# A new order of steps inside a pair of attention units, and 512-column matmuls ahead of the scores in two attentions

## The chip, the cores and the metric

One core of a Trainium2 chip. The metric is the device time in microseconds of one launch of the whole program; for the kernel before it is the median of three runs. TensorE has two levels of clock, 1.2 and 2.4 GHz. The profile gives the granted clock as a share of full speed: 0.50 is 1.2 GHz throughout, 1.00 is 2.4 GHz throughout.

## The reference, cut to what matters

The program is a vision tower in float32: 32 images of 37 tokens (36 patches and one class token), 192 channels, 12 heads. Tokens go through a patch embedding and four layers:

```python
h = _L0_tok_ref(x, ...)                                   # patches @ W + b + pos, class token
h = _layernorm(h + _L0_attn_ref(h, ...))                  # attention whose scores are mixed with their neighbours
h = _layernorm(h + _L0_ffn_ref(h, ...))                   # causal attention, then 8 experts with a capacity
h = _layernorm(h + _L1_attn_ref(h, ...))                  # attention without its diagonal, + h
h = _layernorm(h + _L1_ffn_ref(h, ...))                   # four T5 layers
...
for i in range(L):                                        # L = 4, H = 12, DK = 64
    nx = t5_layer_norm(h, ln1[i])
    q, k, v = nx @ attn_q[i], nx @ attn_k[i], nx @ attn_v[i]
    attn = jax.nn.softmax(q @ k.T + bias, axis=-1)        # for each head
    h = h + (attn @ v) @ attn_o[i]
    nx = t5_layer_norm(h, ln2[i])
    y = relu(nx @ ffn_wi[i]) @ ffn_wo[i]                  # layers 1 and 3 add 2 of 8 experts
    h = h + y
```

So there are seven attentions in a row of twelve stages: one with neighbours, one causal, one without the diagonal (heads of 16 channels each), and four T5 attentions (heads of 64 channels).

## The kernel before, in words

The tokens are cut into 11 groups of three images (111 tokens, `TG`). Stages follow each other as `att 0`, `att 1` (causal), `ffn 0`, `att 2` (diagonal), then four times `att`, `ffn` for T5. Four engines run the same list of steps, `PROGRAM`, each doing its own part of a step: TensorE (PE) its matmuls, VectorE (DVE), ScalarE (ACT) and GpSimd (POOL) what follows. Each engine works through its part strictly in the order of that list and waits on semaphores for the others. So the place of a step in the list sets what stands behind what on every engine. The list is written out by functions; `att_order` (line 276) makes it for all attentions but the first.

In an attention the twelve heads of a group are cut into four units of three heads, and two units make a pair; there are 22 pairs in a stage. The steps are:

- `S` (scores of a pair): PE fills both banks of `ps_score` (line 1042, and in the causal and the diagonal attention a mask by a bfloat16 matmul at line 1037). DVE then shifts each unit: in T5 it adds the bias (line 1423), takes the negated maximum (1425) and adds it (1426). The result is in `prob`.
- `E`: ACT applies the exponential to `prob` (line 1246), both units of the pair, one after the other.
- `PT`: PE transposes a unit of `prob` into the single bank `ps_pt` (line 983), ACT copies it to `probt` (line 1251).
- `PV`: PE multiplies the pair's `probt` by `v` into `ps_o` (line 1064); DVE divides (lines 1440 and 1444) into `o`.
- `OT` and `Y`: the transposed output (line 1073, copy by ACT at line 1230) and its projection (line 1084, DVE adds it to `x` and starts a norm, which POOL ends, lines 1321 to 1351).
- `A`: PE transposes the normed rows (line 887, in the diagonal attention 881), ACT rounds them (lines 1183, 1184), DVE makes the low part (lines 1513, 1516).
- `QK` and `V`: projections from the split input, five matmuls each (lines 1009 and 1022), copied out by ACT (lines 1216 and 1223). `QK` is made for a block of three groups at once: 336 columns.

`ps_proj` has two banks, which `QK`, `V`, `OT` and `Y` take in turn.

`att_order` is a pipeline over pairs. For pair n it lists the scores of n, the exponentials of n, the two transposes of pair n-1, and the `PV` of pair n-2. All other steps of the group (`att_fill`, line 225) are a flat list that is spread evenly over the gaps behind `E`, each `PT` and `PV`:

```python
steps += [("S", g, p), ("E", g, p)]
steps += [("PT", h, 2 * q), ("PT", h, 2 * q + 1)]
steps.append(("PV", *divmod(n - 2, 2)))
```

A `W1` step (a weight load of the next stage, rounded by ACT and split by DVE) and the gathers of an expert stage before (`GAT` on POOL, `COMB` on DVE) are among the fill.

Of the kernel before, what the change touches and what calls it, by code (L numbers as in the profile page):

```python
# [8 lines left out]
ACT = mybir.ActivationFunctionType  # L9
# [23 lines left out]
E = 8  # L33
# [188 lines left out]
    return out  # L222


def att_fill(a, g, last_stage, follower):

    s = ATTS[a]
    ffn_next = follower[0] == "ffn"
    fill = []
    if last_stage in COMBINED and g < G:  # L230
        for c in (3 + 2 * g, 4 + 2 * g):
            if c < G:
                fill.append(("prev", ("COMB", c)))
                if c + GAT_RING < G:
                    fill.append(("prev", ("GAT", c + GAT_RING)))
    if g < G:
        b = BLOCK_OF[g]
        i = g - BLOCKS[b][0]
        if b + 1 < NB:
            g0, n = BLOCKS[b + 1]  # L240
            if i == 1:
                fill += [("A", x) for x in range(g0 + 2, g0 + n)]
                fill += [("QK", b + 1, j) for j in range(s.qk // 2)]
            elif i == 2:
                fill += [("QK", b + 1, j) for j in range(s.qk // 2, s.qk)]
    if 2 <= g:
        fill.insert(0, ("OT", g - 2, s.vparts - 1))
    if g + 1 < G:
        fill += [("V", g + 1, j) for j in range(s.vparts)]
    if 2 <= g:  # L250
        fill.append(("Y", g - 2))
    if a == DIAG and g >= 3:
        fill.append(("N2", g - 3))
    if ffn_next and 3 <= g < G:
        fill.append(("next", ("A", g - 3)))
        if follower[1] in SPARSE and g >= 4:
            fill.append(("next", ("L", g - 4)))
            if g >= 5:
                fill.append(("next", ("CNT", g - 5)))
    if g < G and i == 0 and b + 1 < NB:  # L260
        fill += [("A", x) for x in range(g0, min(g0 + 2, g0 + n))]
    if not ffn_next and g == G - 1:
        fill += [("next", ("A", x)) for x in range(3)]
    if not ffn_next and g == G:
        fill += [("next", x) for x in first_block(follower[1])]
    r = LOAD0[follower]
    if a == DIAG:
        fill += {2: [("W1", r)], 9: [("W1", r + 1)], 10: [("W1", r + 2)]}.get(g, [])
    elif g == (2 if a == CAUSAL else 9):
        fill.append(("W1", r))  # L270
    if s.t5 and 1 <= g:
        fill.append(("OT", g - 1, 0))
    return fill


def att_order(a, last_stage, follower):

    out = first_block(a) if last_stage[0] == "ffn" else []
    pairs = 2 * G
    for n in range(pairs + 2):  # L280
        g, p = divmod(n, 2)
        if p == 0:
            fill = att_fill(a, g, last_stage, follower)
            count, given, gap = len(fill), 0, 0
# [8 lines left out]
        for x in steps:  # L293
            out.append(x)
            if x[0] == "S":
                continue
            gap += 1
            upto = min(-(-count * gap // 8), count)
            out += fill[given:upto]
            given = max(given, upto)  # L300
        if p == 1:
            out += fill[given:]
            given = count
    last = ATTS[a].vparts - 1
    out += fill[given:] + [("OT", G - 1, last), ("Y", G - 1)]
    if a == DIAG:
        out += [("N2", g) for g in range(G) if ("N2", g) not in out]
    return out
# [226 lines left out]
def tower(nc, patches, tok_w, consts, young, rows, gains, gates_w, head_scale, bias_src, edge,  # L535
          aw_neigh, wo_all, w1_all, w2_all, out, rows_in, rows_out):
    with ExitStack() as ctx:
# [306 lines left out]
        def _(pe):  # L844
# [141 lines left out]
            def att_step(st, step):  # L986
# [39 lines left out]
                elif kind == "S":  # L1026
# [137 lines left out]
        def _(act):  # L1164
# [33 lines left out]
            for st, step in PROGRAM:  # L1198
# [35 lines left out]
                elif kind == "E":  # L1234
                    _, g, u = step
                    a = st[1]
                    for e in range(1 if a == NEIGH else 2):
                        v = u if a == NEIGH else 2 * u + e
                        n = SCORE[(st, "S", g, u) if a == NEIGH else (st, "S", g, u, e)]

                        if ATTS[a].t5:
                            act.wait_ge(shifted, unit(a - T5, g, v) + 1)
                        else:
                            act.wait_ge(score_taken[n % 2], n // 2 + 1)
                        at = unit(a, g, v) % 4
                        act.activation(prob[:, at, :, :], prob[:, at, :, :], ACT.Exp).then_inc(prob_ready, 1)  # L1246
                elif kind == "PT":
                    _, g, u = step
                    n = unit(st[1], g, u)
                    act.wait_ge(pt_full, n + 1)  # L1250
                    act.activation(probt[:, n % 4, :, :], ps_pt[0:TG, 0:3 * TG].rearrange("p (c n) -> p c n", c=3),  # L1251
                                   ACT.Copy).then_inc(pt_taken, 1)
                elif kind == "GATE":
                    gates += 1
                    act.wait_ge(gap_ready, gates)
                    act.activation(egap[:], gap[:], ACT.Exp).then_inc(egap_ready, 1)
                elif kind == "U":
                    bank, taken = take_proj(key)
                    _, i, m = step
                    b = FFN[st[1]][i]  # L1260
                    n = DISPATCH[st[1]].width if b.tile is not None else b.groups[1] * TP
                    act.activation(hid[:, i % 2, m, 0:n], bank[:, 0:n],  # L1262
                                   ACT.Relu if b.tile is None else ACT.Gelu).then_inc(taken, 1)
                elif kind == "X":
                    turned_rows(st, step[1])
                elif kind == "W1":
                    r = step[1]
                    act.wait_ge(w1_raw, 16 * (r + 1))
                    if r >= W_RING:

                        act.wait_ge(proj_full, LAST_PROJ[r - W_RING] + 1)
                    act.activation(w1_hi[:, r % W_RING, :, :], w1_in[:], ACT.Copy).then_inc(w1_rounded, 1)  # L1272
# [589 lines left out]
```

## Time and profile before

| what | value |
|---|---|
| median of 3 runs | 2679.45 us (2669.82 to 2680.93) |
| profiled execution, its own time | 2659.68 us |
| its span | 2657.7 us |
| granted TensorE clock, mean | 0.752 |
| PE busy | 2016.8 us (76%) |
| DVE busy | 1135.4 us (43%) |
| ACT busy | 801.1 us (30%) |
| POOL busy | 727.2 us (27%) |

The profile lists, for stretches of the span, the busy time of each engine and the granted clock; for an engine, how long it sat idle and which instruction ended that; and the instructions in order of time. The name behind an arrow is what the engine had waited for. Engines overlap, so busy shares do not add up to the span.

### The profile page before, as it was taken

The numbers are of one execution on the slowest core, as the hardware profiler recorded it, in microseconds if no ns is written. First come the engines' busy times: TensorE is split into PE (matmuls) and PEld (weight loads), VectorE is DVE, ScalarE is ACT, GpSimd is POOL, SyncE is SP. The second block draws the span as 40 slices with busy tenths as digits, with TensorE's granted clock in tenths as the row PEclk, the third lists the DMA queues.
The fourth block names the chain that finished last, engine by engine and source line by source line (L and its number), as shares of the span: only waits on it lengthen the run. The fifth ranks groups of instructions, "written<-read, shape, count | busy, mean of one in ns | idle before, by whom it ended". The sixth has DMA issues, their size and how long they took to land.

```text
span 2657.7 us, 35685 instructions
## 1 busy us (share of the span) xinstructions
PE 2016.8 (76%) x12440; PEld 1851.9 (70%) x12440; DVE 1135.4 (43%) x3201; ACT 801.1 (30%) x1907; POOL 727.2 (27%) x1831
## 2 busy tenths in 40 slices
PE   7984888868388767778777789966777967778991
PEld 7983777768267666668666788855666866778891
DVE  2531434443344434444445543434444444454436
ACT  1221332223122233233333234422332333324440
POOL 3561412220553421125212220044211611131003
PEclk8795555579555577678877699987767988769995
DMA  3094000035000000001000036630000100004651
GB/s 100 17 286 143 1 12 8 14 94 167 23 15 1 25 9 1 1 13 34 12 1 11 11 124 199 195 98 11 1 1 13 45 1 1 11 11 157 200 165 42
DMA packets 77414, 151.03 MB, mean 57 GB/s; under 512 B 6345, under 2 KB 56627, under 8 KB 77142
## 3 DMA queue, kind: packets, MB, share of 16 engines
q1 hardware_dynamic: 70902, 136.49, 16.3%
q0 software_dynamic: 6336, 12.26, 1.6%
q8 instruction: 103, 1.69, 0.3%
q14 instruction: 73, 0.59, 0.1%
HBM read 108.67 MB, written 41.05 MB: 56 GB/s over the span
## 4 chain that ended last, share of the span: by engine, by line
PE 45%; DVE 21%; issue 18%; ACT 5%; POOL 5%; DMA 3%; SPq 2%; DVEq 0%; POOLq 0%; ACTq 0%
PE ps_proj L1009 8%; PE ps_o L1064 7%; PE ps_proj L1084 6%; DVE prob L1426 5%; DVE negmax L1425 5%; PE ps_score L1042 4%; PE ps_score L1155 4%; PE ps_pt L983 3%; DVE prob L1423 3%; PE ps_proj L1138 3%; PE ps_proj L1022 2%; ACT prob L1246 2%; PE ps_proj L936 2%; DMA w_in<-w_all_dram 2%; SPq L812 2%
## 5 line engine op out<-in xcount | busy, mean ns | idle before, releaser
L1321 POOL TENSOR_SCALAR tmp<-rs,var 111x1 f32<-111x1 f32 x462 | 168.1, 364 | 1218.5 <-DVE rs L1397 1187.2
L983 PE MATMUL ps_pt<-const,prob 111*111 111x111 f32 x924 | 208.6, 352 | 161.8 <-ACT probt L1251 161.2
L1246 ACT ACTIVATE prob<-prob 111x333 f32<-111x333 f32 x308 | 148.0, 481 | 591.2 <-DVE prob L1426 591.2
L1155 PE MATMUL ps_score<-w,hid 128*112 128x192 f32 (+2 forms) x1680 | 309.0, 336 | 10.6 <-DVE x L1700 6.2
L983 PEld LDWEIGHTS ps_pt<-const,prob 111*111 111x111 f32 x924 | 176.6, 252 | 185.0 <-ACT prob L1246 176.2
L1155 PEld LDWEIGHTS ps_score<-w,hid 128*112 128x112 f32 (+2 forms) x1680 | 280.3, 182 | 13.2 <-DVE x L1700 7.5
L1064 PEld LDWEIGHTS ps_o<-v,probt 111*111 111x111 f32 x1584 | 250.2, 251 | 3.3 <-issue 2.6
L1064 PE MATMUL ps_o<-v,probt 111*111 111x65 f32 (+1 forms) x1584 | 247.7, 316 | 0.0
L1262 ACT ACTIVATE hid<-ps_proj 128x224 f32<-128x224 f32 (+2 forms) x360 | 134.1, 382 | 262.9 <-PE ps_proj L1138 262.8
L1309 POOL DMA_INDIRECT tin<-rows_out,idx x66 | 67.2, 1018 | 495.1 <-issue 385.0
L1084 PE MATMUL ps_proj<-wo,ot 128*111 128x192 f32 (+1 forms) x616 | 165.3, 427 | 25.9 <-ACT ot L1230 13.8
L1251 ACT ACTIVATE probt<-ps_pt 111x333 f32<-111x333 f32 x308 | 137.5, 446 | 137.3 <-PE ps_pt L983 134.2
L1042 PE MATMUL ps_score<-qk 64*111 64x111 f32 (+1 forms) x1584 | 154.7, 346 | 23.6 <-DVE prob L1423 13.6
L1009 PE MATMUL ps_proj<-xa_hi,w_hi 128*128 128x336 f32 (+1 forms) x240 | 112.3, 468 | 79.4 <-DVE xb L1516 41.1
L1042 PEld LDWEIGHTS ps_score<-qk 64*111 64x111 f32 (+1 forms) x1584 | 125.6, 239 | 61.6 <-issue 57.9
L1084 PEld LDWEIGHTS ps_proj<-wo,ot 128*111 128x111 f32 (+1 forms) x616 | 133.1, 237 | 41.9 <-issue 24.8
L1425 DVE TENSOR_REDUCE negmax<-ps_score 111x3 f32<-111x333 f32 x132 | 66.6, 504 | 210.0 <-PE ps_score L1042 131.2
L1216 ACT ACTIVATE qk<-ps_proj 128x336 f32<-128x336 f32 (+1 forms) x228 | 96.5, 425 | 191.7 <-PE ps_proj L1009 191.7
L1440 DVE RECIPROCAL rden<-ps_o 111x6 f32<-111x6 f32 (+1 forms) x121 | 24.9, 206 | 286.6 <-PE ps_o L1064 275.5
L1322 POOL TENSOR_SCALAR tmp<-tmp,rs 111x1 f32<-111x1 f32 x462 | 133.2, 288 | 46.9
L1272 ACT ACTIVATE w_hi<-w_in 128x1536 fp32r<-128x1536 f32 x66 | 97.9, 1483 | 115.6 <-DMA w_in<-w_all_dram 115.6
L1536 DVE TENSOR_TENSOR w_lo<-w_in,w_hi 128x768 fp32r<-128x768 f32 x66 | 63.8, 966 | 155.7 <-ACT w_hi L1272 155.5
(214 smaller groups left out, 4444.9 us busy)
## 6 DMA issues: line engine op xcount, KB each, us to landing
w_in<-w_all_dram SPq DMA_DIRECT2D x66, 768.0 KB, 4.4
w<-w_all_dram SPq DMA_DIRECT2D x50, 576.0 KB, 5.0
rows_in<-w_lo SPq DMA_DIRECT2D x1, 12320.0 KB, 62.6
rows_out<-w_lo SPq DMA_DIRECT2D x1, 9240.0 KB, 85.7
tin<-rows_in SPq DMA_DIRECT2D x36, 224.0 KB
rows_out<-tout SPq DMA_DIRECT2D x36, 168.0 KB
patch<-patches_dram SPq DMA_DIRECT2D x11, 333.0 KB, 3.0
wo<-wo_all_dram SPq DMA_DIRECT2D x6, 576.0 KB, 3.9
```

The source lines that it names most:

```text
L983: last = pe.transpose(ps_pt[0:TG, i * TG:(i + 1) * TG], prob[:, n % 4, i, :], ident)
L1009: last = pe.matmul(bank[:, 0:n * TP], w[:, slot, c, at:at + 128], src, start=(i == 0), stop=(i == len(terms) - 1))
L1042: ins = pe.matmul(bank[0:TG, i * TG:(i + 1) * TG], qk[at:at + s.rows, b % 2, c, t0:t0 + TG], qk[at:at + s.rows, b % 2, s.chunks + c, t0:t0 ...
L1064: last = pe.matmul(ps_o[0:TG, h // 6, col:col + s.d + 1], probt[:, unit(a, g, u) % 4, i, :], v[:, g % 3, h, :], start=True, stop=True, ski ...
L1084: last = pe.matmul(bank[0:TG, 0:C], ot[0:n, g % 2, c, :], w[0:n, c, :], start=(c == 0), stop=(c == len(parts) - 1))
L1155: last = pe.matmul(bank[0:n, 0:C], hid[:, i % 2, m, at:at + n], w2[:, slot, m, :], start=(m == 0), stop=(m == FC - 1))
L1246: act.activation(prob[:, at, :, :], prob[:, at, :, :], ACT.Exp).then_inc(prob_ready, 1)
L1251: act.activation(probt[:, n % 4, :, :], ps_pt[0:TG, 0:3 * TG].rearrange("p (c n) -> p c n", c=3), ACT.Copy).then_inc(pt_taken, 1)
L1262: act.activation(hid[:, i % 2, m, 0:n], bank[:, 0:n], ACT.Relu if b.tile is None else ACT.Gelu).then_inc(taken, 1)
L1321: link(pool.tensor_scalar(t, r, r, v, ALU.mult, ALU.mult))
L1322: link(pool.tensor_scalar(t, t, -3.0, r, ALU.add, ALU.mult))
L1425: link(dve.tensor_reduce(negmax[:], scores, AX.X, ALU.max, negate=True))
```

## The change

Two things.

The order inside a pair is rewritten, for the six attentions from the causal one on. `att_fill` no longer returns a flat list, it returns six named slots for a group (three for each of its two pairs), and each fill step has its fixed slot. `E` is now a step of a single unit. For pair n the list now reads: scores of n; first transpose of n-1; slot; second transpose of n-1; slot; first exponential of n; `PV` of n-2; slot; second exponential of n.

And in the causal attention (all groups) and the diagonal one (groups 0 to 8), PE runs four matmuls of 128 x 512 ahead of each pair's scores, and twelve ahead of the first pair's. They read a ready weight block of the next stage and write the first score bank, whose content the mask matmul then overwrites. That makes 2 x 12 + 38 x 4 = 176 of them; nothing reads what they compute.

```diff
+COMB_AT = {0: ((3, 0), (4, 2)), 1: ((5, 1), (6, 5)), 2: ((7, 3),), 3: ((8, 1),), 4: ((9, 1),), 5: ((10, 1),)}
...
 def att_fill(a, g, last_stage, follower):
...
+    slots = [[] for _ in range(6)]
+    if 2 <= g:
+        slots[0].append(("OT", g - 2, s.vparts - 1))
     if g < G:
...
         if b + 1 < NB:
             g0, n = BLOCKS[b + 1]
+            if i == 0:
+                slots[3].append(("A", g0))
             if i == 1:
-                fill += [("A", x) for x in range(g0 + 2, g0 + n)]
-                fill += [("QK", b + 1, j) for j in range(s.qk // 2)]
-            elif i == 2:
-                fill += [("QK", b + 1, j) for j in range(s.qk // 2, s.qk)]
+                for k, x in zip((0, 3), range(g0 + 1, g0 + n)):
+                    slots[k].append(("A", x))
+            if i:
+                sixth = s.qk // 6
+                for k, slot in enumerate((4, 5) if i == 1 else (1, 2, 4, 5)):
+                    first = (k if i == 1 else k + 2) * sixth
+                    slots[slot] += [("QK", b + 1, j) for j in range(first, first + sixth)]
+    if g + 1 < G:
+        for j in range(s.vparts):
+            slots[(1, 4)[j]].append(("V", g + 1, j))
     if 2 <= g:
-        fill.insert(0, ("OT", g - 2, s.vparts - 1))
...
+        slots[2].append(("Y", g - 2))
...
     if s.t5 and 1 <= g:
-        fill.append(("OT", g - 1, 0))
-    return fill
+        slots[5].append(("OT", g - 1, 0))
+    return slots
...
-        steps = []
+            slots = att_fill(a, g, last_stage, follower)
         if n < pairs:
-            steps += [("S", g, p), ("E", g, p)]
-        if 1 <= n <= pairs:
-            h, q = divmod(n - 1, 2)
-            steps += [("PT", h, 2 * q), ("PT", h, 2 * q + 1)]
+            out.append(("S", g, p))
+        for k in range(2):
+            if 1 <= n <= pairs:
+                h, q = divmod(n - 1, 2)
+                out.append(("PT", h, 2 * q + k))
+            out += slots[3 * p + k]
+        if n < pairs:
+            out.append(("E", g, 2 * p))
         if n >= 2:
-            steps.append(("PV", *divmod(n - 2, 2)))
...
+            out.append(("PV", *divmod(n - 2, 2)))
+        out += slots[3 * p + 2]
+        if n < pairs:
+            out.append(("E", g, 2 * p + 1))
...
+DENSE = {CAUSAL: 4, DIAG: 4}
...
+                    if a in DENSE and g < (9 if a == DIAG else G):
+
+                        full = w1_hi[:, LOAD0[st] % W_RING, :, :].rearrange("p c n -> p (c n)")
+                        for _ in range(DENSE[a] * (3 if p == 0 and g == 0 else 1)):
+                            pe.matmul(banks[0], full[:, 0:128], full[:, 0:512], start=True, stop=True,
+                                      skip_group_check=True)
```

In the changed kernel lines are shifted: the scores are line 1050, the transposes 985, the exponential 1252, the copy of a transpose 1257, the block transpose's rounding 1191 and 1192, the copies of `ot`, `v` and `qk` 1238, 1231 and 1224; the added matmuls are line 1041.

How ACT's order moves, in the first T5 attention, from the last pair of group 2 into group 3. Before:

```order
L1251 ACTIVATE probt<-ps_pt 111x333
L1230 ACTIVATE ot<-ps_proj 128x333
L1246 ACTIVATE prob<-prob 111x333 x2
L1230 ACTIVATE ot<-ps_proj 128x333
L1251 ACTIVATE probt<-ps_pt 111x333
L1223 ACTIVATE v<-ps_proj 111x6x64
L1251 ACTIVATE probt<-ps_pt 111x333
L1223 ACTIVATE v<-ps_proj 111x6x64
L1246 ACTIVATE prob<-prob 111x333 x2
```

The same place in the changed kernel:

```order
L1238 ACTIVATE ot<-ps_proj 128x333
L1252 ACTIVATE prob<-prob 111x333
L1257 ACTIVATE probt<-ps_pt 111x333
L1238 ACTIVATE ot<-ps_proj 128x333
L1257 ACTIVATE probt<-ps_pt 111x333
L1231 ACTIVATE v<-ps_proj 111x6x64
L1252 ACTIVATE prob<-prob 111x333 x2
```

Before, both exponentials of the new pair stand ahead of the two copies of transposes and of what lies between them; now they stand behind.

How PE's order moves, in the causal attention, at the first pair of group 2. Before:

```order
L1064 MATMUL ps_o<-v,probt 111x17 x6
L1037 MATMUL ps_score<-maskb,identb 111x333 x2
L1042 MATMUL ps_score<-qk 111x111 x6
L1073 MATMUL ps_proj<-const,o 128x111
L1073 MATMUL ps_proj<-const,o 64x111
L983 MATMUL ps_pt<-const,prob 111x111 x3
```

The same place in the changed kernel:

```order
L1041 MATMUL ps_score<-w_hi 128x512 x4
L1045 MATMUL ps_score<-maskb,identb 111x333 x2
L1050 MATMUL ps_score<-qk 111x111 x6
L985 MATMUL ps_pt<-const,prob 111x111 x3
L1081 MATMUL ps_proj<-const,o 128x111
L1081 MATMUL ps_proj<-const,o 64x111
L985 MATMUL ps_pt<-const,prob 111x111 x3
```

The four new matmuls stand right ahead of the mask, and the first transpose is moved to stand right behind the scores, ahead of the output transposes.

## Rows read from the trace of the kernel before

**Rows 1.** The page: PE's busy share, and its granted clock in 40 slices.
```profile
PE 2016.8 (76%) x12440; PEld 1851.9 (70%) x12440; DVE 1135.4 (43%) x3201; ACT 801.1 (30%) x1907; POOL 727.2 (27%) x1831
...
PEclk8795555579555577678877699987767988769995
```

**Rows 2.** Stretches by attention: start:end, length, busy per engine, clock, DMA share, GB/s.
```profile
302.00:530.00 228.00, 190.71 (x1002) 162.43 (x1002) 92.42 (x300) 62.66 (x172) 57.20 (x141) 0.54 0.03 10
700.00:925.00 225.00, 179.33 (x939) 147.81 (x937) 103.33 (x294) 64.84 (x164) 102.10 (x275) 0.54 0.03 9
943.00:1190.00 247.00, 172.67 (x1074) 157.93 (x1073) 104.12 (x258) 75.94 (x192) 43.19 (x121) 0.73 0.02 6
1275.00:1525.00 250.00, 180.53 (x1175) 165.99 (x1172) 120.08 (x340) 79.10 (x198) 51.32 (x125) 0.77 0.02 6
1785.00:2040.00 255.00, 177.03 (x1073) 162.10 (x1072) 115.77 (x298) 77.75 (x192) 68.94 (x184) 0.73 0.02 7
2125.00:2375.00 250.00, 181.93 (x1175) 167.28 (x1172) 120.10 (x340) 79.13 (x198) 50.77 (x124) 0.76 0.02 6
```

**Rows 3.** Who PE waited for, 302 to 2375 us: total, times, longest.
```profile
PE ps_pt L983 <- ACT probt L1251: 112.3, 53, 6.0
PE ps_turn L887 <- POOL xn L1351: 58.4, 13, 11.7
PE ps_proj L1009 <- DVE xb L1516: 41.1, 13, 4.5
...
PE ps_proj L1009 <- ACT ot L1230: 37.1, 18, 2.7
PE ps_proj L1022 <- ACT qk L1216: 29.6, 17, 2.2
...
PE ps_proj L1084 <- ACT ot L1230: 13.1, 10, 2.7
PE ps_proj L1084 <- ACT v L1223: 12.1, 6, 2.0
...
PE ps_proj L1022 <- ACT ot L1230: 5.2, 4, 1.8
```

**Rows 4.** Timeline, one pair of the first T5 attention: start, duration, engine, instruction, idle before.
```profile
1009.04 0.84 PE L1042 MATMUL ps_score<-qk 64*111 64x111 f32 x12
...
1011.85 0.48 ACT L1246 ACTIVATE prob<-prob 111x333 f32<-111x333 f32 x1 [2.25 <-DVE prob L1426]
...
1013.46 0.48 ACT L1246 ACTIVATE prob<-prob 111x333 f32<-111x333 f32 x1 [1.13 <-DVE prob L1426]
...
1014.18 0.44 ACT L1251 ACTIVATE probt<-ps_pt 111x333 f32<-111x333 f32 x1
...
1014.76 0.87 PE L983 MATMUL ps_pt<-const,prob 111*111 111x111 f32 x3 [2.78 <-ACT probt L1251]
```

**Rows 5.** Timeline of PE: the same matmuls at either clock, start and duration.
```profile
1388.82 0.32 PE L1009 MATMUL ps_proj<-xb,w_hi 128*128 128x336 f32 x1
1388.98 0.32 PE L1009 MATMUL ps_proj<-xb,w_lo 128*128 128x336 f32 x1
...
1389.81 0.48 PE L1009 MATMUL ps_proj<-xb,w_hi 128*128 128x336 f32 x1
1390.09 0.48 PE L1009 MATMUL ps_proj<-xb,w_lo 128*128 128x336 f32 x1
...
1393.31 1.29 PE L1064 MATMUL ps_o<-v,probt 111*111 111x65 f32 x12
```

**Rows 6.** Timeline of PE: `PV` of a T5 pair at the low clock.
```profile
1032.78 2.37 PE L1064 MATMUL ps_o<-v,probt 111*111 111x65 f32 x12
```

**Rows 7.** Stretches of 50 us: first attention, first expert stage, second T5 attention.
```profile
250.00:300.00 50.00, 50.00 (x228) 46.02 (x229) 18.25 (x56) 11.11 (x30) 23.58 (x68) 0.50 0.00 1
...
600.00:650.00 50.00, 48.14 (x329) 47.82 (x326) 18.45 (x31) 21.35 (x40) 0.00 (x0) 1.00 0.51 165
...
1300.00:1350.00 50.00, 35.63 (x243) 32.66 (x239) 21.16 (x51) 16.26 (x40) 7.52 (x21) 0.85 0.00 1
```

More of the change, by code:

```diff
@@ L228, in att_fill @@
     ffn_next = follower[0] == "ffn"
[L229 to L235, printed above, removed]
+    slots = [[] for _ in range(6)]
+    if 2 <= g:
+        slots[0].append(("OT", g - 2, s.vparts - 1))
     if g < G:
@@ L240, in att_fill @@
             g0, n = BLOCKS[b + 1]
+            if i == 0:
+                slots[3].append(("A", g0))
             if i == 1:
-                fill += [("A", x) for x in range(g0 + 2, g0 + n)]
-                fill += [("QK", b + 1, j) for j in range(s.qk // 2)]
-            elif i == 2:
-                fill += [("QK", b + 1, j) for j in range(s.qk // 2, s.qk)]
-    if 2 <= g:
-        fill.insert(0, ("OT", g - 2, s.vparts - 1))
-    if g + 1 < G:
-        fill += [("V", g + 1, j) for j in range(s.vparts)]
@@ L250, in att_fill @@
-    if 2 <= g:
-        fill.append(("Y", g - 2))
+                for k, x in zip((0, 3), range(g0 + 1, g0 + n)):
[8 more added lines that the diff above has]
+            slots[(1, 4)[j]].append(("V", g + 1, j))
@@ L252, in att_fill @@
+    if 2 <= g:
+        slots[2].append(("Y", g - 2))
+    if last_stage in COMBINED and g < G:
+        for c, k in COMB_AT.get(g, ()):
+            slots[k].append(("prev", ("COMB", c)))
+            if c + GAT_RING < G:
+                slots[k].append(("prev", ("GAT", c + GAT_RING)))
     if a == DIAG and g >= 3:
-        fill.append(("N2", g - 3))
+        slots[4].append(("N2", g - 3))
     if ffn_next and 3 <= g < G:
-        fill.append(("next", ("A", g - 3)))
+        slots[3].append(("next", ("A", g - 3)))
@@ L256, in att_fill @@
         if follower[1] in SPARSE and g >= 4:
-            fill.append(("next", ("L", g - 4)))
+            slots[2].append(("next", ("L", g - 4)))
             if g >= 5:
-                fill.append(("next", ("CNT", g - 5)))
-    if g < G and i == 0 and b + 1 < NB:
-        fill += [("A", x) for x in range(g0, min(g0 + 2, g0 + n))]
+                slots[5].append(("next", ("CNT", g - 5)))
     if not ffn_next and g == G - 1:
-        fill += [("next", ("A", x)) for x in range(3)]
+        for x in range(3):
+            slots[1 + x].append(("next", ("A", x)))
@@ L264, in att_fill @@
     if not ffn_next and g == G:
-        fill += [("next", x) for x in first_block(follower[1])]
+        slots[3] += [("next", x) for x in first_block(follower[1])]
     r = LOAD0[follower]
     if a == DIAG:
-        fill += {2: [("W1", r)], 9: [("W1", r + 1)], 10: [("W1", r + 2)]}.get(g, [])
+        slots[5] += {2: [("W1", r)], 9: [("W1", r + 1)], 10: [("W1", r + 2)]}.get(g, [])
     elif g == (2 if a == CAUSAL else 9):
-        fill.append(("W1", r))
+        slots[5].append(("W1", r))
     if s.t5 and 1 <= g:
-        fill.append(("OT", g - 1, 0))
@@ L282, in att_order @@
         if p == 0:
-            fill = att_fill(a, g, last_stage, follower)
-            count, given, gap = len(fill), 0, 0
-        steps = []
+            slots = att_fill(a, g, last_stage, follower)
         if n < pairs:
-            steps += [("S", g, p), ("E", g, p)]
-        if 1 <= n <= pairs:
-            h, q = divmod(n - 1, 2)
-            steps += [("PT", h, 2 * q), ("PT", h, 2 * q + 1)]
-        if n >= 2:
-            steps.append(("PV", *divmod(n - 2, 2)))
[L293 to L303, printed above, removed]
+            out.append(("S", g, p))
[6 more added lines that the diff above has]
+            out.append(("E", g, 2 * p))
+        if n >= 2:
+            out.append(("PV", *divmod(n - 2, 2)))
+        out += slots[3 * p + 2]
+        if n < pairs:
+            out.append(("E", g, 2 * p + 1))
     last = ATTS[a].vparts - 1
-    out += fill[given:] + [("OT", G - 1, last), ("Y", G - 1)]
+    out += [("OT", G - 1, last), ("Y", G - 1)]
     if a == DIAG:
@@ L1236, in _ @@
                     a = st[1]
[L1237 to L1246, printed above, removed]
+                    n = SCORE[(st, "S", g, u) if a == NEIGH else (st, "S", g, u // 2, u % 2)]
+                    if ATTS[a].t5:
+                        act.wait_ge(shifted, unit(a - T5, g, u) + 1)
+                    else:
+                        act.wait_ge(score_taken[n % 2], n // 2 + 1)
+                    at = unit(a, g, u) % 4
+                    act.activation(prob[:, at, :, :], prob[:, at, :, :], ACT.Exp).then_inc(prob_ready, 1)
                 elif kind == "PT":
```

## The prediction

> **What bounds the kernel now.** I read the share of the engines and the clock first, then the attentions one by one, then who PE waits for in them, then one pair in order of time. The page: PE is busy for 2016.8 us of 2657.7, and no other engine for half of it, so PE and its waits set the end; its clock dips in exactly the slices that hold attentions [rows 1]. The stretches: the causal and the diagonal attention take 228 and 225 us, with PE busy for 190.71 and 179.33 at a granted clock of 0.54, that is almost wholly at 1.2 GHz. The four T5 attentions take 247, 250, 255 and 250 us; PE is busy for 172.67, 180.53, 177.03 and 181.93 at 0.73 to 0.77 [rows 2]. Together these six stretches are 1455 us, with PE idle for 83.0 us in the first two (453.0 less 370.0) and 289.8 in the other four (1002.0 less 712.2). Two things are to be had there: the idle time, and the half speed.
>
> The waits: of the idle time the largest single one is PE's transposes waiting for ACT's copy of the one before, 112.3 us. With the other waits that ACT ends (37.1, 29.6, 13.1, 12.1 and 5.2) it makes 209.4 us [rows 3]. ACT is not busy at all: 76 to 79 us of 250 [rows 2]. The pair in order of time says why. The scores start at 1009.04. ACT's next instruction in its list is the exponential, which it can start only at 1011.85 and, for the second unit, at 1013.46, since DVE must shift both units first. The copy of a transpose that had long been there follows at 1014.18, and PE, with its two projection banks full and its one transpose bank occupied, sits idle for 2.78 us until 1014.76 [rows 4]. So in each pair ACT's queue stands for some 4 us behind exponentials that nobody needs yet (they are used one pair later).
>
> **The change part by part.**
>
> *The exponentials.* Copies of transposes, of `qk`, `v` and `ot` that PE needs at once now stand ahead of them. The first exponential comes after two transposes and two slots, the second after `PV` and another slot. By then DVE has done its shift in most pairs (4.4 us from the start of the scores to the second exponential [rows 4]), and if not, PE has that much work ahead of it. A wait of ACT costs PE only when two more projections pile up. What stays: the second transpose still needs the copy of the first (0.44 us [rows 4] and the way there and back), and a slot between them is sometimes empty or a short `OT`. I take four fifths of the 209.4 us: **168 us**. The bounds are 0, if the exponential only blocks at its new place, and 209.
>
> *The other moved steps.* A group's first pair has `OT`, `V` and `Y`, its second `A`, `V`, `OT`. `QK` was halved over the second and third group of a block; now the third has two thirds, the second one third, the first none, as before. `A` of a block's last group stands one slot ahead of the first `QK`, which needs DVE's low part, and DVE has the pair's two shifts ahead of it. That wait is there already (41.1 us in 13 waits), as is the one for POOL's norms (58.4 in 13) [rows 3]; I leave both as they are. The gathers, the combining steps behind an expert stage and the weight loads keep their groups and move by at most a group's worth; POOL (102.10 of 225 us in its fullest stretch [rows 2]) and SP's queue have room.
>
> *The T5 clock.* A dense PE should be granted the high clock for longer. What it is worth: five matmuls of 336 columns follow each other at 0.28 us at the low clock and at 0.16 at the high one; a `PV` takes 2.37 us and 1.29 [rows 5, 6]. So at full clock PE needs 0.55 of its time at the low one. A granted share c is a share 2c - 1 of the time at the high clock; the time factor is 1 - 0.45(2c - 1). At today's mean, 0.75, it is 0.78. I take 0.92 for a PE without its ACT waits (factor 0.62), since 0.85 is had now in a stretch where PE is busy for 35.63 of 50 us [rows 7]. Busy time goes from 712 to 570: **142 us** less. Bounds: 0 (the clock stays) and 208 (1.00 throughout).
>
> *The 176 dense matmuls.* By 512/336 of those distances one costs 0.43 us at the low clock and 0.24 at the high one [rows 5]; all of it is on PE's path, ahead of the scores, so 42 to 75 us for all. What they could buy is the clock of those two attentions. Busy share does not give it: the first attention has PE busy for 50.00 of 50 us at 0.50, an expert stage, all wide matmuls, 48.14 at 1.00 [rows 7]. What these attentions lack against the latter is wide matmuls, and four of 512 columns once a pair (now 10 us long, then some 7) are the widest there are. I take 0.90 there (factor 0.64, against 0.96 today at 0.54): busy time goes from 370 to 246, **124 us** less, and the dense ones cost 176 x 0.274 = **48 us** more. Bounds: 0 less with 75 more, and 158 less with 42 more. The Trainium skill, in "TensorE: Matmul & The Clock Gate", section "Back-to-back issue gap", prices a matmul of N columns at N/1.2 ns cold and N/2.4 + 2.5 ns warm. By that the 176 would cost 45 us at the mix above instead of 48; the cold rows agree (0.28 us for 336), the warm ones are some 10 ns longer.
>
> *What is late next.* DVE needs 460.1 us in the T5 stretches [rows 2], or 5.2 us for each of 88 pairs, and does not get faster. PE would need 570/88 = 6.5 on the mean, but in the groups without `QK` (5 of 11, 40 pairs in four stages) it comes down to DVE's 5.2, and each jitter is a wait. I charge 0.75 us for each of the 40: **30 us**. In the causal and diagonal attention PE needs (246 + 48)/44 = 6.7 a pair, DVE (92.42 + 103.33)/44 = 4.4: no charge.
>
> The sum, against the profiled execution: 2659.7 - 168 - 142 - 124 + 48 + 30 = 2303.7. That execution is 20 us under the median of the runs shown (2679.45) and 10 under the lowest of them (2669.82), so the median should lie a little above the sum: **2310 us**, 14% under the median before.
>
> **The rivals.**
>
> *The T5 clock stays where it is.* The causal and diagonal attention get the dense matmuls, the T5 ones get nothing and still have short idle moments at every pair. For it: the clock falls and rises all through these stages today, and half of the transposes and the `OT` are small. Against it: 0.85 is seen there with PE busy for 71%. Then 142 us are not gained and the charge of 30 falls away: 2310 + 112 = 2422. The Trainium skill speaks for this one: on the same page, "A second HAM failure mode: psum-queue depth-cycling" says that micro-idles between groups of matmuls, as the PSUM banks are cycled, make the clock oscillate. By that rule the two projection banks and the one transpose bank would keep it oscillating; the trace agrees that it oscillates now, at 0.73 to 0.77.
>
> *Everything falls into place.* Clock 1.00, all ACT waits gone, DVE keeps up: 208 + 158 + 209 - 42 = 533 less, 2127; with half of the 30 and something for the stages' ends, 2150 to 2200. For it: no engine but PE is needed for more than 5.2 us a pair. Against it: the waits for POOL and DVE at the block borders stay.
>
> *Four matmuls are too little.* They do not lift the clock of either attention, nor does the T5 clock rise: 168 - 75 = 93 less, 2567, with the offset 2574. For it: the first attention is fully busy at 0.50 [rows 7]. Against it: the twelve ahead of the first pair last 5 us.
>
> *Slower: the exponentials block at their new place.* The second exponential now stands behind the last slot's copies, so the next pair's second transpose, and all copies behind it, wait for it; PE's 112.3 us of waits change their name. With the clock unmoved, the dense matmuls add 75 us: 2660 + 75 + 7 = 2742. It decides as soon as less than 75 of the 209 us of waits go (36%) and the clock stays. Against it: the second exponential has from 1009.04 to 1013.46 of DVE's work to wait for, and PE's work of a pair is longer than that.
>
> *The change does not do what it says*, the time staying within 0.5%: two effects would have to cancel to 13 us.
>
> **How the numbers follow.** Forecast 0.47; all in place 0.20; T5 clock stays 0.20; no clock anywhere 0.07; slower 0.04; no change 0.02. The range takes the first three and their unknowns: down to 2180, near the upper end of "all in place", and up to 2450, past "T5 clock stays" by 28 us for a few more waits. That leaves out 0.13 above and part of a case below. Faster by over 0.5%: 0.94; within 0.5% (about what a measurement can tell from no change): 0.02; slower: 0.04.
>
> **What the profile of the changed kernel would show.** Right: the wait of the transposes for ACT's copy under 40 us in all (from 112.3), pairs of about 7 us in the causal and diagonal attention (from 10) at a clock near 0.9, T5 stretches of some 190 us at 0.92 (from 250), 176 matmuls of 512 columns at 0.24 us from one to the next. DVE would be named more often in PE's waits. Wrong: a clock under 0.6 in the causal attention (the dense matmuls bought nothing), T5 at 0.75, or PE waiting for ACT's exponential where it waited for the copy. What would make the prediction wrong most is the clock, which carries 266 of the 356 us.

## The result, and the profile after

The changed kernel takes 2394.56 us (median; 2387.28 to 2397.76) beside 2674.64 us of the kernel before: a ratio of 0.8953, 95% interval 0.8914 to 0.8991. The forecast was 2310 us with a range of 2180 to 2450. The direction and the range held; the gain is 280 us where 369 were forecast. The profiled execution took 2387.28 us.

The page of the changed kernel, against [rows 1]:

```profile
span 2385.3 us, 36037 instructions
...
PE 1937.6 (81%) x12616; PEld 1771.9 (74%) x12616; DVE 1135.5 (48%) x3201; ACT 795.7 (33%) x1907; POOL 735.5 (31%) x1831
...
PEclk8995575558966868898988789987889887789995
```

PE is busy for 79 us less, although it runs 176 matmuls more, and DVE and ACT do what they did. For the six attentions I compare stretches that run from the first score matmul of an attention to its last, since the borders of [rows 2] cut some stages short. Before (all six in order, and their sum), columns as in [rows 2]:

```profile
305.10:516.30 211.20, 176.25 (x931) 149.09 (x930) 87.23 (x278) 58.26 (x161) 51.49 (x132) 0.54 0.03 10
703.60:915.20 211.60, 170.38 (x889) 140.08 (x890) 97.94 (x283) 57.90 (x149) 97.08 (x261) 0.53 0.03 10
945.80:1192.50 246.70, 173.14 (x1085) 158.83 (x1086) 105.91 (x266) 74.65 (x187) 43.53 (x122) 0.73 0.02 6
1274.50:1513.80 239.30, 172.56 (x1135) 158.75 (x1136) 113.81 (x319) 76.03 (x190) 46.59 (x116) 0.78 0.02 6
1787.20:2042.60 255.40, 177.43 (x1085) 162.73 (x1084) 117.50 (x306) 76.66 (x189) 69.21 (x185) 0.73 0.02 7
2124.50:2363.80 239.30, 173.95 (x1137) 160.04 (x1136) 113.85 (x320) 76.03 (x190) 46.04 (x116) 0.77 0.02 6
sum 1403.50, PE 1043.70 PEld 929.52 DVE 636.23 ACT 419.53 POOL 353.94; mean PE 173.95 PEld 154.92 DVE 106.04 ACT 69.92 POOL 58.99
```

The same stretches of the changed kernel, all six in order:

```profile
294.60:508.30 213.70, 189.39 (x1018) 154.56 (x1017) 86.56 (x278) 56.41 (x159) 48.61 (x124) 0.63 0.03 10
696.50:868.70 172.20, 156.23 (x959) 125.55 (x960) 97.12 (x279) 58.03 (x151) 94.86 (x254) 0.72 0.04 12
896.80:1070.00 173.20, 141.30 (x1086) 129.19 (x1086) 103.75 (x258) 73.69 (x186) 45.06 (x121) 0.89 0.03 7
1152.30:1347.20 194.90, 162.00 (x1139) 150.43 (x1139) 114.52 (x324) 75.14 (x188) 47.43 (x117) 0.82 0.02 7
1620.60:1802.50 181.90, 145.96 (x1085) 133.48 (x1084) 115.80 (x298) 75.70 (x188) 70.86 (x184) 0.85 0.03 8
1882.50:2082.20 199.70, 166.72 (x1140) 154.72 (x1139) 114.54 (x324) 75.33 (x188) 47.49 (x117) 0.79 0.02 7
sum 1135.60, PE 961.61 PEld 847.93 DVE 632.29 ACT 414.30 POOL 354.31; mean PE 160.27 PEld 141.32 DVE 105.38 ACT 69.05 POOL 59.05
```

What is to be seen: 267.9 of the 272.4 us by which the span shrank lie in these stretches. PE's busy time fell by 82.1 us, its idle time from 359.8 to 174.0, by 185.8. The causal attention gained nothing at all (211.2 and 213.7 us), the diagonal one 39 us, and the four T5 ones 74, 44, 74 and 40.

Who PE waited for, 292 to 2093 us of the changed kernel, against [rows 3]:

```profile
PE ps_turn L889 <- DVE xb L1522: 59.9, 19, 5.9
PE ps_pt L985 <- ACT probt L1257: 35.6, 93, 0.6
...
PE ps_score L1050 <- DVE logit L1623: 22.7, 14, 1.6
PE ps_proj L1011 <- DVE xb L1522: 14.9, 9, 3.0
...
PE ps_score L1041 <- DVE logit L1623: 6.2, 7, 1.2
...
PE ps_pt L985 <- ACT prob L1252: 3.6, 3, 1.7
PE ps_proj L1092 <- ACT ot L1238: 3.1, 5, 0.6
```

The wait for the copy of a transpose fell from 112.3 us in 53 waits to 35.6 in 93: many short ones, 0.6 us at most, which is the way of a copy out of the one bank and back. A pair of the second T5 attention in order of time shows the new order at work, against [rows 4]:

```profile
1195.05 0.84 PE L1050 MATMUL ps_score<-qk 64*111 64x111 f32 x12 [0.35 <-ACT qk L1224]
1195.82 0.55 PE L985 MATMUL ps_pt<-const,prob 111*111 111x111 f32 x3
...
1196.40 0.45 ACT L1257 ACTIVATE probt<-ps_pt 111x333 f32<-111x333 f32 x1 [0.79 <-PE ps_pt L985]
...
1196.99 0.51 PE L985 MATMUL ps_pt<-const,prob 111*111 111x111 f32 x3 [0.34 <-ACT probt L1257]
...
1198.81 0.87 ACT L1252 ACTIVATE prob<-prob 111x333 f32<-111x333 f32 x2
...
1201.44 0.84 PE L1050 MATMUL ps_score<-qk 64*111 64x111 f32 x12
```

ACT copies right behind the transpose, PE is back at its second transpose after 0.34 us idle (2.78 before), both exponentials come later without a wait of ACT's own, and the pair takes 6.4 us.

A new wait is in the list, for DVE's copy of the gate's logits. The 22.7 us at the scores are the second and the fourth T5 attention, seven waits in each; the 6.2 us at the added matmuls are the causal one. Two pairs of the causal attention, of which the second has the wait:

```profile
380.49 1.91 PE L1041 MATMUL ps_score<-w_hi 128*128 128x512 f32 x4
382.20 0.71 PE L1045 MATMUL ps_score<-maskb,identb 111*111 111x333 bf16 x2
...
389.70 0.24 PE L1109 MATMUL ps_score<-gate_lo,xb 128*111 128x8 f32 x1
...
390.83 0.17 DVE L1623 COPY logit<-ps_score 111x8 f32<-111x8 f32 x1
...
391.14 1.16 PE L1041 MATMUL ps_score<-w_hi 128*128 128x512 f32 x4 [1.21 <-DVE logit L1623]
392.14 0.45 PE L1045 MATMUL ps_score<-maskb,identb 111*111 111x333 bf16 x2
```

The logits of the next expert stage use a score bank. In the fixed slots they stand right ahead of the next pair's scores, and DVE has the projection `Y` of the same slot to add and to start its norm from before it can free the bank. The rows also give the distance from one added matmul to the next: 0.43 us (1.71 us for four) at 380.49 and 0.25 us (1.00 us for four) at 391.14.

### The profile page after: what moved, and what is told of

It is laid out like the page before. It is cut to its first block, busy times and chain, and to the rows that moved or that the text cites. A ratio compares the mean times of both kernels' runs of the same rounds, so it can differ in the third digit from the quotient of the medians.

```text
span 2385.3 us, 36037 instructions
## 1 busy us (share of the span) xinstructions
PE 1937.6 (81%) x12616; PEld 1771.9 (74%) x12616; DVE 1135.5 (48%) x3201; ACT 795.7 (33%) x1907; POOL 735.5 (31%) x1831
## 4 chain that ended last, share of the span: by engine, by line
PE 51%; issue 23%; DVE 13%; POOL 4%; DMA 3%; ACT 3%; SPq 2%; another core or an unknown queue 0%; DVEq 0%; POOLq 0%; ACTq 0%
PE ps_proj L1011 9%; PE ps_o L1072 7%; PE ps_pt L985 5%; PE ps_proj L1092 5%; PE ps_score L1050 4%; PE ps_proj L1024 4%; PE ps_score L1163 4%; PE ps_proj L1146 3%; PE ps_score L1041 2%; DMA w_in<-w_all_dram 2%; PE ps_proj L938 2%; SPq L814 2%; DVE prob L1432 2%; DVE negmax L1431 2%; ACT probt L1257 1%
## 5 line engine op out<-in xcount | busy, mean ns | idle before, releaser
L1327 POOL TENSOR_SCALAR tmp<-rs,var 111x1 f32<-111x1 f32 x462 | 181.7, 393 | 846.0 <-DVE rs L1403 814.5
L985 PEld LDWEIGHTS ps_pt<-const,prob 111*111 111x111 f32 x924 | 147.1, 222 | 128.8 <-issue 62.5
L1072 PEld LDWEIGHTS ps_o<-v,probt 111*111 111x111 f32 x1584 | 224.3, 224 | 1.4 <-issue 0.5
L1072 PE MATMUL ps_o<-v,probt 111*111 111x65 f32 (+1 forms) x1584 | 217.6, 292 | 0.0
L1050 PE MATMUL ps_score<-qk 64*111 64x111 f32 (+1 forms) x1584 | 137.2, 316 | 39.9 <-DVE logit L1623 22.7
L1050 PEld LDWEIGHTS ps_score<-qk 64*111 64x111 f32 (+1 forms) x1584 | 111.3, 212 | 74.1 <-issue 71.8
L1092 PE MATMUL ps_proj<-wo,ot 128*111 128x192 f32 (+1 forms) x616 | 139.8, 376 | 3.7 <-ACT ot L1238 3.7
L1429 DVE TENSOR_TENSOR prob<-ps_score,relbias 111x333 f32<-111x333 f32 x176 | 88.8, 505 | 86.2 <-PE ps_score L1050 81.6
L889 PE MATMUL ps_turn<-const,xn 111*128 111x111 f32 x220 | 51.6, 326 | 94.8 <-DVE xb L1522 59.9
L1092 PEld LDWEIGHTS ps_proj<-wo,ot 128*111 128x111 f32 (+1 forms) x616 | 111.6, 202 | 14.2 <-issue 12.7
```

What stands on the lines that cost most here:

```text
L985: last = pe.transpose(ps_pt[0:TG, i * TG:(i + 1) * TG], prob[:, n % 4, i, :], ident)
L1050: ins = pe.matmul(bank[0:TG, i * TG:(i + 1) * TG], qk[at:at + s.rows, b % 2, c, t0:t0 + TG], qk[at:at + s.rows, b % 2, s.chunks + c, t0:t0 ...
L1072: last = pe.matmul(ps_o[0:TG, h // 6, col:col + s.d + 1], probt[:, unit(a, g, u) % 4, i, :], v[:, g % 3, h, :], start=True, stop=True, ski ...
L1092: last = pe.matmul(bank[0:TG, 0:C], ot[0:n, g % 2, c, :], w[0:n, c, :], start=(c == 0), stop=(c == len(parts) - 1))
L1327: link(pool.tensor_scalar(t, r, r, v, ALU.mult, ALU.mult))
```

## The experiments

The ratios are to the kernel before, run on the same chip at the same time. The first four runs share one chip, e5 to e8 a second and e9 to e11 a third, so runs of different chips are compared by their ratios.

**Each half alone.** The order without the dense matmuls (e1_order_only):

```diff
-DENSE = {CAUSAL: 4, DIAG: 4}
+DENSE = {}
```

> The changed kernel without its 176 dense matmuls. Theory A (the order carries the gain; the dense matmuls only pay for themselves, since the causal stretch has a clock of 0.62 and takes as long as before): 2375 to 2405 us, the causal attention's 22 pairs in about 200 us at 0.50 to 0.55, the diagonal ones in about 190 at 0.55. Theory B (the dense matmuls carry part of the gain through the clock): 2420 to 2470 us, with the diagonal attention back at 205 us or more. The T5 attentions stay at about 190 us each under both.

And the kernel before with the dense matmuls and nothing else (e2_dense_only):

```diff
+DENSE = {CAUSAL: 4, DIAG: 4}
...
+                    if a in DENSE and g < (9 if a == DIAG else G):
+                        full = w1_hi[:, LOAD0[st] % W_RING, :, :].rearrange("p c n -> p (c n)")
+                        for _ in range(DENSE[a] * (3 if p == 0 and g == 0 else 1)):
+                            pe.matmul(banks[0], full[:, 0:128], full[:, 0:512], start=True, stop=True,
+                                      skip_group_check=True)
```

> The kernel before with the 176 dense matmuls and its old order. Theory A: they cost about what they take at the low clock and give back a little, 2675 to 2750 us. Theory B: the clock of the two attentions rises above 0.7 and the time falls, 2600 to 2650 us. The T5 attentions stay at 235 us for 22 pairs.

Measured: the order alone 2370.59 us, ratio 0.8907 (0.8847 to 0.8967); the dense matmuls alone 2731.96 us, ratio 1.0256 (1.0194 to 1.0317), so slower. The stretches of the order alone (causal, diagonal, second and fourth T5, sum of six):

```profile
333.70:531.30 197.60, 174.05 (x933) 145.86 (x933) 87.49 (x283) 56.92 (x159) 49.58 (x128) 0.56 0.03 11
717.50:890.70 173.20, 151.20 (x891) 123.49 (x892) 97.56 (x279) 58.76 (x151) 94.71 (x254) 0.62 0.04 12
...
1176.00:1371.90 195.90, 162.44 (x1138) 150.95 (x1139) 114.82 (x325) 75.47 (x188) 47.32 (x118) 0.81 0.02 7
...
1906.80:2106.50 199.70, 166.69 (x1138) 154.61 (x1139) 114.50 (x323) 75.43 (x188) 46.69 (x116) 0.79 0.02 7
sum 1123.70, PE 944.64 PEld 839.98 DVE 633.92 ACT 416.33 POOL 353.60; mean PE 157.44 PEld 140.00 DVE 105.65 ACT 69.39 POOL 58.93
```

And causal and diagonal attention of the dense matmuls alone, with PE's wait for the copies in that run:

```profile
312.80:557.60 244.80, 205.72 (x1015) 170.21 (x1014) 86.12 (x273) 58.14 (x161) 50.95 (x126) 0.57 0.03 9
747.30:976.20 228.90, 183.15 (x957) 148.81 (x958) 98.37 (x283) 56.63 (x148) 97.07 (x261) 0.59 0.03 9
...
PE ps_pt L984 <- ACT probt L1258: 120.4, 54, 6.0
```

So the order carries the whole gain: its interval and that of the full change overlap, and the other half alone makes the kernel slower. In the old order the dense matmuls make the two attentions 51 us longer (473.7 against 422.8), and the clock rises by 0.03 and 0.06 only. Theory A holds on both sides; the median of the order alone is 4 us below its range, and the diagonal attention took 173 us where 190 were expected. The profiled execution of the order alone took 2399.89 us, 29 more than the median; that time was lost ahead of these stretches, as the section on the hardware shows.

**One edit instead of the new list.** The old list with the exponentials behind the transposes (e3_exp_late), and a second version with them behind `PV` (e6_exp_last):

```diff
-            steps += [("S", g, p), ("E", g, p)]
+            steps.append(("S", g, p))
         if 1 <= n <= pairs:
             h, q = divmod(n - 1, 2)
             steps += [("PT", h, 2 * q), ("PT", h, 2 * q + 1)]
+        if n < pairs:
+            steps.append(("E", g, p))
         if n >= 2:
             steps.append(("PV", *divmod(n - 2, 2)))
```

> The kernel before with one edit: a pair's exponentials stand behind its two transposes instead of ahead of them; fill steps spread as before, no dense matmuls. If ACT's queue behind the exponentials is the cause, this one edit brings most of the gain of the order: 2420 to 2500 us and PE's waits for the copy of a transpose fall from 112 us to under 50. If the fixed slots and the split of the exponential are what matters: above 2580 us.

> As e3_exp_late, with the exponentials moved one place further, behind PV. If what counts is only that ACT's copies stand ahead of them, the time is as in e3_exp_late, 2340 to 2365 us. If the exponentials can come too late (the rival by which I gave slower a chance), PE waits for prob at the next pair's transposes for over 30 us and the time is above 2380.

Measured: 2352.24 us, ratio 0.8832 (0.8784 to 0.8880), and behind `PV` 2342.48 us, 0.8836 (0.8746 to 0.8927). This one edit of three lines gives more than the whole change does: the first interval lies wholly under that of the change. The sum of the six stretches, and the wait for the copies, with the exponentials behind the transposes:

```profile
sum 1107.70, PE 924.08 PEld 824.39 DVE 635.48 ACT 417.29 POOL 354.01; mean PE 154.01 PEld 137.40 DVE 105.91 ACT 69.55 POOL 59.00
...
PE ps_pt L985 <- ACT probt L1253: 16.1, 39, 1.0
```

The wait fell to 16.1 us and the time went lower than I had expected for this edit (2420 to 2500). The six stretches became 295.8 us shorter: idle time fell from 359.8 to 183.6 us, and PE's busy time for the same matmuls from 1043.7 to 924.1. So 120 us of the gain are busy time, and it goes with the clock: in the four T5 stretches that is 0.81 to 0.85 here and was 0.73 to 0.78.

The cause is ACT's queue behind the exponentials. One thing goes with the edit: a gap for fill steps that stood between the scores and the first transpose on PE now stands behind the second transpose. No run separates the two. That PE's own order is the cause is unlikely, since in [rows 4] the second transpose waits for a copy that stands behind both exponentials in ACT's list, and an earlier first transpose would not bring this copy forward. That the exponentials could come too late, my rival for a slower kernel, falls: one place further back changes nothing that can be told, and PE waits for an exponential for 4.9 us in nine waits there.

**Where the fixed slots lose.** The T5 attentions that an expert stage follows, the second and the fourth, took 195 and 200 us in the slots and 186 and 187 us in the run with the one edit; the first and the third took 173 and 182 against 178 and 191. The former two have the new wait for the logits, 11 us in each. The logits and the counts were moved one slot ahead, in the order without dense matmuls (e5_gate_earlier, and the same kernel again as e11_gate_again); in e10_logits_only only the first of the two edits was made:

```diff
-            slots[2].append(("next", ("L", g - 4)))
+            slots[1].append(("next", ("L", g - 4)))
...
-                slots[5].append(("next", ("CNT", g - 5)))
+                slots[4].append(("next", ("CNT", g - 5)))
```

> The new order without dense matmuls, and with the gate's logits and counts of the next expert stage one slot earlier, so that they no longer stand right ahead of the next pair's scores, with which they share the two score banks. Theory A (the 22.7 us that the scores wait for DVE's copy of the logits, in 14 waits, are why the causal, second and fourth T5 attentions are slower in the fixed slots than in run e3_exp_late): 2345 to 2365 us, the second and fourth T5 attention at 186 to 190 us (from 196 and 200), the causal one under 192. Theory B (that wait only hides another, DVE's own work): no change, 2370 us.

> The new order without dense matmuls, with the logits one slot earlier and the counts left where they are, right ahead of the scores. If the logits alone are the 22.7 us of waits and what hangs on them: within 10 us of e11_gate_again. If the counts cost as much: halfway, 2340 to 2350 us.

> The same kernel as e5_gate_earlier, on the chip of its neighbours for a direct comparison: 2310 to 2335 us.

Measured: 2320.39 us, ratio 0.8716 (0.8626 to 0.8806); the same kernel again, on another chip, 2350.68 us, 0.8802 (0.8755 to 0.8850); the logits alone 2336.41 us, 0.8744 (0.8693 to 0.8794). No wait of the scores for the logits is left in any of the three. The second and the fourth T5 attention of e5_gate_earlier:

```profile
1131.80:1309.60 177.80, 150.63 (x1138) 138.26 (x1139) 113.53 (x321) 75.30 (x188) 48.55 (x113) 0.88 0.03 8
1841.80:2019.60 177.80, 150.64 (x1140) 138.24 (x1139) 113.56 (x321) 75.29 (x188) 48.55 (x113) 0.88 0.03 8
```

Those two went from 195.9 and 199.7 us (order alone) to 177.8 each. Only 6 us of that is idle time in either, since other waits grew when this one went; the rest is PE's busy time for the same matmuls, 162.4 and 166.7 down to 150.6, at a clock of 0.88 instead of 0.81 and 0.79. In the other four runs with the logits moved these two attentions take 177.8 to 182.5 us, so this difference is not that of a single execution. So seven waits of 1.6 us in 22 pairs, 11 us in all, cost more than themselves: 18 and 22 us. The theory for this run had put the 22.7 us on three attentions, and they are on two; the time came out 25 us under its range. With the logits alone the time lies 14 us under the repeat, outside the 10 us expected and on the side where the counts cost nothing; PE waits for them for 8.6 us there and 2.3 in the repeat, and the medians do not show it. The repeat missed its expected range of 2310 to 2335 us by 16; its causal and diagonal attention, against those of the first run of the same kernel:

```profile
296.50:485.70 189.20, 173.38 (x934) 145.11 (x933) 87.53 (x283) 56.92 (x159) 48.36 (x123) 0.56 0.04 11
672.90:846.30 173.40, 149.99 (x891) 122.30 (x892) 97.45 (x279) 58.74 (x151) 94.22 (x254) 0.63 0.04 12
```
```profile
297.90:499.70 201.80, 185.72 (x932) 155.24 (x933) 87.42 (x283) 56.79 (x159) 48.69 (x123) 0.51 0.03 10
687.10:882.70 195.60, 176.86 (x892) 144.29 (x892) 97.19 (x279) 58.05 (x151) 92.94 (x254) 0.51 0.03 11
```

The first pair is the first run, the second the repeat: the same program, 35 us apart in two attentions, with the clock. Differences of up to that size between two profiles of these two stretches therefore show nothing by themselves.

**How much dense.** Eight a pair instead of four; eight in the diagonal attention alone, with the gate moved; four with the gate moved; and two a pair in the T5 attentions, none elsewhere (160 in all: 68 pairs with two, and four first pairs with six):

```diff
-DENSE = {CAUSAL: 4, DIAG: 4}
+DENSE = {CAUSAL: 8, DIAG: 8}                      # e4_dense8
+DENSE = {DIAG: 8}                                 # e7_gate_earlier_diag8
+DENSE = {CAUSAL: 4, DIAG: 4}                      # e9_gate_dense4
+DENSE = {a: 2 for a in range(T5, NATT)}           # e8_t5_dense2, groups 0 to 8
```

> The changed kernel with eight dense matmuls ahead of each pair instead of four (24 ahead of the first), 352 in all. If four are too few to hold the clock, eight hold it: 0.85 or more in both attentions, and 2330 to 2380 us. If the clock is not the limit there, each costs 0.24 to 0.43 us and the time rises by 40 to 75 us to 2435 to 2470.

> e5_gate_earlier with eight dense matmuls a pair in the diagonal attention alone (160), none in the causal one. The diagonal attention took 162 us with eight of them and 173 without: if that is the dense matmuls' doing, 8 to 12 us below e5_gate_earlier. If they only break even there too, as e4_dense8 against e1_order_only says of the whole, the same within 5 us.

> The changed kernel, its 176 dense matmuls kept, with the gate's logits and counts one slot earlier. If the edit is worth 50 us (e5_gate_earlier against e1_order_only) whatever the dense matmuls do: 2340 to 2355 us. Against e11_gate_again it tells what the dense matmuls cost in the better order: 0 to 30 us more, by theory A 20.

> The new order with two dense matmuls ahead of each pair's scores in groups 0 to 8 of the four T5 attentions (76 pairs and 4 first ones: 160 matmuls), none in the causal and diagonal ones. If the T5 clock of 0.79 to 0.86 is worth buying: it rises to 0.92 or more and the time falls to 2335 to 2360 us. If it is break-even there as well: 2365 to 2385 us, the 35 us of added matmuls given back by shorter ones.

Measured: eight 2372.40 us, 0.8940 (0.8879 to 0.9001); diagonal alone 2326.66 us, 0.8747 (0.8683 to 0.8810); four with the gate moved 2336.35 us, 0.8737 (0.8679 to 0.8795); T5 2394.10 us, 0.8981 (0.8912 to 0.9051). Causal and diagonal attention with eight, and with four and the gate moved:

```profile
294.60:501.30 206.70, 176.82 (x1100) 143.57 (x1101) 86.53 (x278) 55.92 (x159) 47.56 (x122) 0.81 0.03 10
694.40:856.60 162.20, 143.13 (x1027) 115.89 (x1028) 97.13 (x279) 57.15 (x151) 94.43 (x254) 0.91 0.04 13
```
```profile
316.70:505.30 188.60, 170.65 (x1016) 138.78 (x1017) 86.51 (x278) 56.50 (x159) 46.84 (x120) 0.71 0.04 11
694.50:853.10 158.60, 140.79 (x959) 113.88 (x960) 97.20 (x279) 57.97 (x151) 95.05 (x254) 0.80 0.04 13
```

With eight the clock is 0.81 and 0.91 (0.85 in both was expected), and PE is busy there for 319.9 us against 325.3 in the order alone. The added matmuls are 99.7 us of that, so PE's other work took 105 us less: price and gain cancel, within the 35 us by which two executions differ. With four in the changed kernel they are 64.5 of 345.6 us, and the other work took 44 us less. In ratios, every pair with and without them overlaps: 0.8953 and 0.8940 against 0.8907 in the slots as given, 0.8747 and 0.8737 against 0.8716 and 0.8802 with the gate moved. In the T5 attentions the clock rises from 0.85, 0.81, 0.86 and 0.79 to 0.91, 0.88, 0.88 and 0.85, and their stretches grow from 752.9 us (order alone) to 761.6. The T5 run ends above the upper end of its break-even range, 2385. Eight in the diagonal attention ended 6 us above e5_gate_earlier on the same chip, where 8 to 12 less was hoped for. Only four with the gate moved could be a gain: all its executions (2318.80 to 2339.55) lie under all of the repeat without dense matmuls on the same chip (2345.93 to 2365.18). But the run with the logits alone, also without dense matmuls and on that chip, took 2326.37 to 2340.41, so these runs don't show it as one, nor the 0 to 30 us more that were expected.

## Why the prediction was right or wrong

*The waits for ACT: right.* I took away 168 of 209.4 us; left of them, with the new wait for the exponential, are 46 (35.6, 3.6, 3.1, and two of 2.1 and 1.9 for `qk`), so 163 went. That the single edit of the exponentials' place takes the same waits away (21 us are left of the 209.4), and more time than the whole change, shows this cause, with the reservation on PE's order made there.

*The charge of 30 us for DVE: not seen.* Idle time fell by 186 us, more than the ACT waits. DVE's low part is waited for as long as before (74.8 us in the two largest rows, 69.6 before), but the wait for POOL's norms fell from 58.4 to 34.9. Why the charge didn't show is not settled. The cost of the other moved steps, which I set at nothing, was 28.9 us of waits for the logits (22.7 and 6.2) and, through the clock, more. The paragraph on the other moved steps does not name the logits at all; it looked at groups and queues, and not at what a fixed slot puts right ahead of the scores, with whose two banks the logits share a ring. By the ratios, moving them is worth some 28 to 51 us without the dense matmuls (0.8907 against 0.8802 and 0.8716) and 58 with them (0.8953 against 0.8737). The smaller of these is not clear of the noise, as its interval and that of the order alone just meet; the others are.

*The T5 clock: the step that was mis-sized first.* I took 0.92, for 142 us of busy time. Measured are 0.89, 0.82, 0.85 and 0.79, and 81 us (697.1 to 616.0). The step from the clock to the busy time held: with the measured clocks the prediction's formula gives some 629 us (an estimate). What was too high is the 0.92 itself. The waits for the logits explain only a part of that, since without them the second and the fourth T5 attention stand at 0.85 to 0.88. The rival "the T5 clock stays" had priced the other end; the truth lies between.

*The dense matmuls: the step that failed.* I took a clock of 0.90 for 124 us, less 48 for the matmuls: 76 us net. Measured is 0.63 and 0.72, and busy time went from 346.6 to 345.6: 1 us net, and even that is not their doing, since the order alone has 325.3. So the 76 us were not had, and the forecast was missed mainly by them and by the 61 us of the T5 clock. With eight the clock came, for 111.2 us of PE's busy time in the 352 where the 176 took 70.5. "Four matmuls are too little" was right on the clock in the old order, 0.57 and 0.59, where the whole kernel became 72 us slower than before. The price held: 70.5 us lie in the 42 to 75, though above the 48 that I took at a clock of 0.90. No price decided here: what was missing was what the clock gives back for it.

The Trainium skill's formula in "TensorE: Matmul & The Clock Gate", section "Back-to-back issue gap", gives 0.427 us cold and 0.216 warm for 512 columns. The trace of the changed kernel agrees at the low clock (0.43) and stands above it at the high one (0.25).

In numbers: in the six stretches busy time fell by 82 us instead of 218, idle time by 186 instead of 138. Together that is 88 us less than forecast. Outside the stretches the execution became 4.5 us shorter, and 84 us remain between the sum (2303.7) and the profiled execution (2387.3). The forecast was so near because 48 us more of idle time went than I had taken, which no step of the prediction had foreseen: that part is luck.

*The rivals.* Slower: PE waited 3.6 us in three waits for an exponential, and moving it further back cost nothing, so this fell. All in place: not reached, neither by the change nor by its order with the logits moved, 2320 us. T5 clock stays: it rose from 0.73 to 0.78 before to 0.79 to 0.89. The Trainium skill, in "TensorE: Matmul & The Clock Gate", section "A second HAM failure mode: psum-queue depth-cycling", describes a clock that oscillates by short idle moments between groups of matmuls. The trace agrees in so far as the mean clock of every T5 stretch stays between the two levels, and that it rose where the waits went; that the cycling of the banks is what does it, no run here shows.

## What to carry to other kernels

In an in-order queue, ask of each instruction who needs it next, and put copies that free a bank ahead of work that is needed one stage later: one edit of three lines gave 12%. Then look at what stands right ahead of the step that starts each round, and which ring it shares with it. Matmuls added for the clock alone should be tested by themselves: here none of four, eight and two a pair brought a gain that the noise lets one see, and four in the old order lost 2.6%. Closing seven waits of 1.6 us in an attention of 22 pairs raised its clock from 0.81 to 0.88 with nothing added.

## What the runs showed of the hardware

What stands ahead of the causal attention, the first attention with it, is the same in the kernel before, the changed one and all the runs, and yet it does not take the same time. The first 290 us of the changed kernel and of the order alone:

```profile
0.00:290.00 290.00, 228.16 (x1509) 211.75 (x1510) 107.49 (x319) 59.94 (x146) 131.29 (x354) 0.77 0.41 125
```
```profile
0.00:290.00 290.00, 229.31 (x1319) 212.63 (x1320) 88.69 (x259) 48.76 (x117) 110.03 (x291) 0.68 0.41 125
```

PE is busy for as long, but gets through 190 matmuls fewer at the lower clock, and the causal attention starts at 333.7 us instead of 294.6. So 39 us between two profiled executions can come from stages that nobody touched.

Two executions of one program without dense matmuls gave the diagonal attention a granted clock of 0.63 and 0.51, and 173.4 and 195.6 us. And the same matmuls of the second T5 attention took PE 162.4 us of busy time with 33 us of idle time between them, and 150.6 with 27: less idle time, and the clock rose from 0.81 to 0.88. What in detail the clock answers to was not settled by these runs.
